# Four ring banks, one-bank score tiles and two-bank maxima in the attention layers of a macaron block stack

## The reference

```python
q, k, v = (split_heads(x @ w) for w in (wq, wk, wv))      # (b, 16, 2048, 8)
scores = jnp.einsum('bhqd,bhkd->bhqk', q, k)
scores = jnp.where(causal, scores, -jnp.inf)
attn = jax.nn.softmax(scores / np.sqrt(HEAD_DIM), axis=-1)
ctx = jnp.einsum('bhqk,bhkd->bhqd', attn, v)
```

## Time and profile before

| what | value |
|---|---|
| median of 3 runs | 1186.41 us (1183.99 to 1186.95) |
| profiled execution, its own time | 1190.67 us |
| its span in the trace | 1188.8 us |
| busy over the span: PE, DVE, ACT | 89%, 83%, 55% |
| first attention layer, quads only | 194.6 to 581.3 us |

### The profile page before, as it was taken

The page is one execution under the profiler, slowest core; times in us unless marked ns, Lnnn a source line. Parts: engine busy times, 40 slices in busy tenths (PEclk is TensorE's granted clock), DMA queues, the critical chain, the costliest instruction groups (busy, mean ns, idle before and its releaser), DMA issues.

```text
span 1188.8 us, 34469 instructions
## 1 busy us (share of the span) xinstructions
PE 1055.3 (89%) x14718; PEld 484.3 (41%) x14718; DVE 987.5 (83%) x2314; ACT 657.2 (55%) x844; POOL 101.2 (9%) x109
## 2 busy tenths in 40 slices
PE   1999977999999999999798848699999999999987
PEld 1455543333333333334446735333333333333436
DVE  8977478999999999987544766899999999998852
ACT  0322223556787777787423213246677778777773
POOL 6111011000000000000042252000000000000000
PEclk9999998999999999999998978899999999999999
DMA  5430043000000000000001023220000000000001
GB/s 162 160 160 1 1 151 100 3 3 3 2 2 2 3 2 3 2 2 4 1 27 46 28 73 96 64 64 3 2 3 3 3 2 2 3 2 3 3 2 36
DMA packets 29492, 36.67 MB, mean 31 GB/s; under 512 B 3694, under 2 KB 26388, under 8 KB 29084
## 3 DMA queue, kind: packets, MB, share of 16 engines
q1 hardware_dynamic: 27228, 29.22, 7.4%
q0 software_dynamic: 2112, 5.25, 1.6%
HBM read 15.29 MB, written 18.87 MB: 29 GB/s over the span
## 4 chain that ended last, share of the span: by engine, by line
PE 48%; DVE 41%; issue 5%; ACT 3%; DMA 1%; another core or an unknown queue 1%; POOL 0%; SPq 0%; DVEq 0%; ACTq 0%; POOLq 0%
DVE part_max L2057 27%; PE psum L1916 12%; PE psum L1937 11%; PE psum L1887 6%; PE psum L518 3%; PE psum L1902 2%; PE psum L1569 2%; ACT hidden L2019 2%; DVE xn L204 2%; PE psum L1964 1%; PE psum L1168 1%; PE psum L542 1%; DVE norm_v L169 1%; PE psum L1943 1%; PE psum L299 1%
## 5 line engine op out<-in xcount | busy, mean ns | idle before, releaser
L2057 DVE TENSOR_REDUCE part_max<-psum 128x1 f32<-128x512 f32 (+3 forms) x1120 | 675.2, 666 | 38.0 <-PE psum L1943 21.9
L2019 ACT ACTIVATE hidden<-psum 128x1024 f32<-128x1024 f32 (+3 forms) x640 | 539.1, 895 | 220.4 <-PE psum L1887 219.5
L1937 PE MATMUL psum<-k_slots,q_slots 128*32 128x512 f16 (+3 forms) x5120 | 389.2, 353 | 27.7 <-DVE part_max L2057 14.9
L1916 PE MATMUL psum<-hidden,v_aug 128*9 128x512 f32 (+3 forms) x2560 | 290.4, 530 | 0.1
L1937 PEld LDWEIGHTS psum<-k_slots,q_slots 128*32 128x32 f16 x5120 | 123.1, 95 | 284.8 <-DVE part_max L2057 200.6
L1887 PE MATMUL psum<-q_slots,k_slots 32*128 32x512 f16 (+3 forms) x1472 | 140.6, 328 | 9.9 <-ACT hidden L2019 7.9
L1943 PE MATMUL psum<-ident_bf,later_keys 128*32 128x128 bf16 (+2 forms) x1408 | 90.3, 247 | 0.0
L518 PE MATMUL psum<-parts,w_parts 128*128 128x512 f16 x384 | 88.6, 381 | 0.6 <-DVE parts L931 0.6
L1887 PEld LDWEIGHTS psum<-q_slots,k_slots 32*128 32x128 f16 x1472 | 42.1, 91 | 99.2 <-ACT hidden L2019 46.4
L1902 PE MATMUL psum<-later_keys,ident_bf 128*32 128x128 bf16 x2048 | 74.8, 223 | 4.4 <-ACT hidden L2019 1.9
L1916 PEld LDWEIGHTS psum<-hidden,v_aug 128*9 128x9 f32 x2560 | 61.8, 90 | 34.3 <-ACT hidden L2019 1.6
(11 more groups left out here) (277 smaller groups left out, 866.1 us busy)
## 6 DMA issues: line engine op xcount, KB each, us to landing
expert_regions<-k_slots SPq DMA_DIRECT2D x2, 4096.0 KB, 17.9
q_slots<-q_rows SPq DMA_DIRECT2D x8, 512.0 KB, 3.9
k_slots<-k_rows POOLq DMA_DIRECT2D x28, 128.0 KB, 4.1
q_slots<-in_L_ffn_W_dram SPq DMA_DIRECT2D x2, 1024.0 KB, 6.7
q_rows<-parts SPq DMA_DIRECT2D x6, 256.0 KB, 2.6
k_rows<-parts SPq DMA_DIRECT2D x6, 256.0 KB, 2.8
q_slots<-expert_regions SPq DMA_DIRECT2D x20, 64.0 KB, 1.8
sorted_rows<-xn SPq DMA_DIRECT2D x5, 256.0 KB, 2.3
```

The costliest lines, as they stand in the source:

```text
L1916: last = pe.matmul(psum[VW * h:VW * h + DH + 1, O_BANK, off:CH], v_aug[:, j, G * g + h, :], probs[:, (2 * n + h // 2) % NP, h % 2, off:CH] ...
L1937: last = pe.matmul(psum[rows32(m), bank, a * w:(a + 1) * w], q_slots[:, g, qb * P + m * SLOT:qb * P + (m + 1) * SLOT], k_slots[:, G * g + ...
L2019: act.activation(probs[:, tile % NP, :, off:CH], psum[:, bank:bank + 2, off:CH], ACT.Exp, scale=scale).then_inc(exp_done, 1)
L2057: dve.tensor_reduce(part_max[:, step_no[s] % 2, h0:h0 + heads, i, kc], psum[:, bank, 0:heads * w].rearrange("p (a k) -> p a k", a=heads), ...
```

## The change

- The ring has 4 banks (4 to 7), the output bank is 3, the score tiles are three of one bank and one head each (banks 0 to 2). The last chunk's values of the projection go through bank 0.
- Units left of the diagonal take two heads and an even pair of neighbouring ring banks; one VectorE instruction reduces both (L2081 in the new file). Where the ring stands at an odd bank, one is left out. In a turn these pairs come first. The products are the same matmuls as before, one head to a bank (L1956).
- ScalarE takes one head at a time: four instructions of 512 columns instead of two of 1024 (L2044).
- TensorE's order in a turn is now: scores of heads 0 and 1, first half of the ring items, scores of heads 2 and 3, `values` of the quad before, second half. Each head's scores wait for the exponentials three tiles back.
- The output bank is cleared one turn later, and TensorE waits for the third chunk's values (`v_ready`) before the first turn.

```diff
-                    heads = CH // unit_width(step, i, kc)
+                    heads = CH // unit_width(step, i, kc) if kc == step[1] else 2
...
-            S_BANKS, O_BANK, RING_BANKS, RING = 0, 4, 5, 3
+            S_TILES, O_BANK, RING_BANKS, RING = 3, 3, 4, 4
...
-                RING_ITEMS.append([("scores", u) for u in units] + [("max", s) for s in turn_max] +
-                                  [("out", s) for s in turn_out])
+                RING_ITEMS.append([("scores", u) for u in sorted(units, key=banks_of_unit, reverse=True)] +
+                                  [("max", s) for s in turn_max] + [("out", s) for s in turn_out])
...
+                    ring_no[item] = ring_slots[0]
+                    ring_slots[0] += banks_of_item(item) + (ring_slots[0] % 2 if banks_of_item(item) == 2 else 0)
+                    ring_end[item] = ring_slots[0]
...
                 def score_tile(q, pr):
...
                         for par in range(2):
+                            tile = G * quad_no[q] + 2 * pr + par
+                            if cols.start == off and not masked and tile >= S_TILES:
+                                pe.wait_ge(exp_done, tile - S_TILES + 1)
                             rows = rows_of(2 * pr + par)
-                            last = pe.matmul(psum[:, S_BANKS + 2 * (tile % 2) + par, cols],
+                            last = pe.matmul(psum[:, tile % S_TILES, cols],
...
-                    if n >= RING:
-                        pe.wait_ge(ring_read, n - RING + 1)
+                    if ring_end[item] > RING:
+                        pe.wait_ge(ring_read, ring_end[item] - RING)
...
+                        for a, m in itertools.product(range(heads) if both else (), range(COLS)):
+                            last = pe.matmul(psum[rows32(m), both, :][:, a, :],
+                                             q_slots[:, g, qb * P + m * SLOT:qb * P + (m + 1) * SLOT],
+                                             k_slots[:, G * g + h0 + a, kc * CH:(kc + 1) * CH], start=True, stop=True)
...
                 pe.wait_ge(*released)
+                pe.wait_ge(proj.v_ready, NCH - 1)
...
                     if q:
                         score_tile(q, 0)
+                    for item in items[:half]:
+                        ring_item(item)
+                    if q:
                         score_tile(q, 1)
                     if q in diagonal:
                         mask_tile(q, 1)
-                    for item in items[:half]:
-                        ring_item(item)
                     if previous:
                         values(previous)
...
-                            act.activation(probs[:, tile % NP, :, off:CH], psum[:, bank:bank + 2, off:CH],
+                            act.activation(probs[:, (2 * n + h // 2) % NP, h % 2, off:CH], psum[:, tile % S_TILES, off:CH],
                                            ACT.Exp, scale=scale).then_inc(exp_done, 1)
...
+                            dve.tensor_reduce(part_max[:, step_no[s] % 2, h0:h0 + heads, i, kc], psum[:, pair_banks(item), :],
+                                              axis=AX.X, op=ALU.max).then_inc(ring_read, slots_of_item(item))
```

More of the change, by code:

```diff
@@ L307, in values @@
                     b = n * BPC + i
-                    last = pe.matmul(psum[:, self.V_BANK, i * D:(i + 1) * D], xn_t[:, b * P:(b + 1) * P],
+                    last = pe.matmul(self.v_bank(n)[:, i * D:(i + 1) * D], xn_t[:, b * P:(b + 1) * P],
                                      self.w_qkv[:, 2, :], start=True, stop=True)
@@ L1890, in score_tile @@
                                              start=not masked, stop=(q not in diagonal or masked) and cols.stop == CH)
-                    if q not in diagonal or masked:
-                        last.then_inc(scores_done, 1)
+                            if cols.stop == CH and (q not in diagonal or masked):
+                                last.then_inc(scores_done, 1)
                 def mask_tile(q, pr):
                     off = first_query(q)
-                    tile = 2 * quad_no[q] + pr
-                    if pr == 0 and tile >= 2:
-                        pe.wait_ge(exp_done, tile - 1)
                     for par in range(2):
+                        tile = G * quad_no[q] + 2 * pr + par
+                        if pr == 0 and tile >= S_TILES:
+                            pe.wait_ge(exp_done, tile - S_TILES + 1)
                         for m in range(COLS):
-                            last = pe.matmul(psum[rows32(m), S_BANKS + 2 * (tile % 2) + par, off:off + P],
+                            last = pe.matmul(psum[rows32(m), tile % S_TILES, off:off + P],
                                              ident_bf[:, rows32(m)], later_keys[:, :], start=(pr == 0), stop=(pr == 1))
-                    if pr == 1:
-                        last.then_inc(scores_done, 1)
+                        if pr == 1:
+                            last.then_inc(scores_done, 1)
                 def values(q):
@@ L1950, in ring_item @@
                     elif kind == "turned":
-                        pe.wait_ge(ring_read, ring_no["out", (NG - 1, what)] + 1)
+                        pe.wait_ge(ring_read, ring_end["out", (NG - 1, what)])
                         for i in range(BPC):
@@ L1954, in ring_item @@
                     elif kind == "project":
-                        pe.wait_ge(ring_read, ring_no["turned", what] + 1)
+                        pe.wait_ge(ring_read, ring_end["turned", what])
                         for i in range(BPC):
@@ L2012, in _ @@
                         off = first_query(q)
-                        for pr in range(2):
-                            tile = 2 * n + pr
+                        for h in range(G):
+                            tile = G * n + h
                             act.wait_ge(scores_done, tile + 1)
-                            if tile >= NP:
-                                act.wait_ge(pv_done, (tile - NP) // 2 + 1)
-                            bank = S_BANKS + 2 * (tile % 2)
-                            act.activation(probs[:, tile % NP, :, off:CH], psum[:, bank:bank + 2, off:CH],
+                            if n >= NP // 2 and h == 0:
+                                act.wait_ge(pv_done, n - NP // 2 + 1)
+                            act.activation(probs[:, (2 * n + h // 2) % NP, h % 2, off:CH], psum[:, tile % S_TILES, off:CH],
                                            ACT.Exp, scale=scale).then_inc(exp_done, 1)
@@ L2050, in _ @@
                         kind, what = item
[L2051 to L2054, removed]
+                        bank = bank_of(item)
+                        dve.wait_ge(ring_full, ring_end[item])
+                        if kind == "scores" and banks_of_item(item) == 2:
+                            s, i, kc, h0, heads = what
+                            dve.tensor_reduce(part_max[:, step_no[s] % 2, h0:h0 + heads, i, kc], psum[:, pair_banks(item), :],
+                                              axis=AX.X, op=ALU.max).then_inc(ring_read, slots_of_item(item))
+                        elif kind == "scores":
                             s, i, kc, h0, heads = what
```

56 lines of the change are left out of this document (32 added, 24 removed).

## The result

The change made the kernel slower: 1360.55 us median (1354.32 to 1365.0) against 1185.58 us (1183.99 to 1186.95), a ratio of 1.1473 with a 95% interval of 1.1423 to 1.1522. Forecast were 1248 us and at most 1287. The direction held; the size was almost three times the 61 us of the sum.

What follows compares the result with a forecast made beforehand. VectorE was taken to bound A, VectorE and TensorE about equally B, TensorE and its waits C. Per layer 0, +21, +9 and opening 0.65 make 30.7; two layers add 61 us to 1186.4, giving 1248 us, range 1218 to 1287.

Steps and rivals of the forecast that it cites:

- Ring of four, read in pairs: VectorE's pair reads in the PSUM ring: 0 where TensorE is later; the other bound 16 us per layer.
- A: First layer's steps 1 to 5, 36 quads in 103.1 us, VectorE 99% busy; forecast 0, between -3 and +5.
- B: First layer's steps 6 to 10, 76 quads in 178.2 us, two engines about equally late; forecast +21 us.
- Scores in two halves: TensorE's split score order: 312 more switches per layer at 0.105 us, and one more pass of 0.216 per full quad.
- The wait of head 3: With three score tiles, head 3 waits for head 0's exponential: 0.22 us in 38 quads of B, 8.4 us.
- C: First layer's last six steps, 48 quads in 105.4 us; forecast +9 us, between +4.5 and +13.
- Exponentials by single heads: ScalarE's full quad goes from 1.84 to 1.98 us; covered, so nothing added; uncovered 22 us per layer.
- Maxima in pairs: VectorE's paired reductions save about 0.066 us each: 192 pairs, 12.7 us of VectorE per layer.
- the ring stalls: Rival, chance 0.13: ring waits add 16 us per layer, giving 1279 us.
- the wait of head 3 is hidden: Rival, chance 0.15: exponentials run ahead, so head 3's wait costs nothing; 61 - 17 = 44, 1230 us.
- TensorE does not bind: Rival, chance 0.05: new switches and passes fall into TensorE's idle time, only the maxima count; 1174 us, or 1165.
- the switch is dearer in new places: Rival, chance 0.07: TensorE's added switches cost half as much again as 0.105 us; 33 us more, 1281 us.

Runs made afterwards that it cites:

- e2: Changed kernel without pairs: every unit is one bank of the ring of four, read by itself; 1288.03 us, ratio 1.0850 to the kernel before.
- e3: Kernel before with only the order of the scores split: heads 0 and 1, first half of ring items, heads 2 and 3; 1262.49 us, ratio 1.0644.
- e8: Changed kernel, ring items waiting only for the last item in their banks, with the old order of four heads' scores together; 1457.41 us, ratio 1.2293.
- e7: Changed kernel, ring items waiting only for the last item in their banks, with each pair read by two reductions; 1324.49 us, against 1322.66 without that edit.
- e5: Changed kernel's deal with pairs first, but each head of a pair filled, read and released as its own ring item; 1303.79 us, ratio 1.0993.
- e10: Changed kernel dealt by two heads, each head its own ring item, units in their own order instead of pairs first; 1294.52 us, ratio 1.0922.

## Why the prediction was wrong in size

**The step that failed** is "Ring of four, read in pairs": "Where TensorE is the later engine VectorE is ahead, so 0", with 16 us per layer as the other bound. The runs show 72 us for both layers, 36 per layer (1360.55 against e2's 1288.03). Three things were priced wrong. The rule by which a left-out bank is counted stands in the code and was told in the description, but the wait that follows from it was not followed through: 38 us. That VectorE starts only when both banks are full, and that TensorE needs both free, was said and then put at 0: 19 us. The bound counted 31 quads of A and B with two pairs; the list of ring items has two or more in 66. And the deal was taken as unchanged, while units dealt by twos and put first cost 16 us. The assumption behind the zero, that one engine is ahead, did not hold in A, where the sum itself had both at 99 and 102 us; A became 23.9 us longer, and 0 was forecast. Nor did it hold in B, which is 11.4 us longer than in e2.

**Scores in two halves** was right as a mechanism and mis-sized. The switches stand in the trace (419.63 to 419.95 and 419.95 to 420.50, 0.10 and 0.12 more than the streams). But the order alone costs 76 us, and 43 were put down for it. In A, 8.7 per layer came where "two engines that close give no gain" had 0; this is with three banks, and with four (e2) the 0 nearly held. In B 22.6 came for 12.6: the slack of 18 us was taken as free to fill, but ring waits stay in it. The starts of neighbouring unit products lie 7.3 us further apart than their streams, summed over B of the kernel before, still 6.6 in e3, and only 0.6 in e2 with its fourth bank.

**The wait of head 3** was right in B and missing in C. The round trip is 1.07 in e8 (1.085). In the changed kernel's first layer head 3 starts more than 0.05 us after head 2 in 41 quads of B, by 0.21 in the median and 8.3 us in all; forecast were 38 quads, 0.22 each and 8.4. In the kernel before and in e3 no quad shows this. But 35 quads of C show it too, with 11.7 us, where the sum had nothing and its upper bound 4. Against e3 the stretches of e2 are -7.7 in A, +4.6 in B and +12.6 in C. So 1288 - 1186 - 76 - 9.5 = 16 us, what three tiles and the fourth bank add to the split and the one-head exponentials, lies near the 17 forecast by luck: a gain in A and a loss in C, neither of them in the sum, nearly cancel.

**Exponentials by single heads**: nothing put down, 9.5 us measured. **Maxima in pairs**: 0.066 each as worked out (two in a row take 2.36 and one 1.23, so they start 1.13 apart, against two times 0.598), and worth at most a few us, as A had no stretch left in which VectorE alone set the time (e7). **Opening**: 0.65 put down per layer; the first exponential starts at 193.8 us against 194.6 before, so no loss shows.

**The rivals.** That the ring stalls had 0.13 and the right mechanism, but half its price: 32 us against 72. That the wait of head 3 is hidden is refuted by the 41 quads. That TensorE does not bind is refuted by e3, where the split alone costs 76 us, and by e2's B. That the switch is dearer in new places is refuted by the 0.10 to 0.12.

The Trainium skill, "TensorEngine Tiling (Array Packing)", Key Properties, says that changing the tiling mode drains TensorE. The trace agrees in that time is lost at each change, 0.10 to 0.12 us; that it is a drain is not shown. The full drain that was estimated with the Trainium skill's page "TensorE: Matmul & The Clock Gate", Single matmul latency, 0.163, does not appear.

## What to carry to other kernels

Follow every wait of a ring through the list of its items before pricing it at nothing: a slot that is left out but counted with its neighbour can make an item wait for the very item ahead of it. Where two engines are about equally late, as in A here, price what couples them more tightly (two banks at once, a coarser deal) above nothing; here it cost more than the edit saved. A saving on an engine counts only if the same edit leaves that engine the later one; here giving 25 us of VectorE back cost about 3. And compare runs at the granted clock: 9 us between two medians here (e5 and e10) were 2 in the stretches at one clock.

## What was not expected of the hardware

A reduction over two neighbouring PSUM banks takes 1.223 us, against 0.681 + 0.53 = 1.21 for one bank's reduction and a second bank's stream: crossing from one bank to the next shows no cost of its own beyond 0.01. And the change between row and column tiles cost the same in all four traces in which its starts were compared (before, after, e2, e3): medians of 0.10 from the last score to unit products and 0.11 back (0.115 in e3), with two score matmuls between as with four.
